# Graph convolution by one-hot products: every summing product split into four of 32 targets, and gathers and sums alternating on TensorE

## The reference, cut to what matters

```python
def gcn_conv(x, W, b, src, dst, n):
    h = x @ W
    deg = jnp.zeros((n,), h.dtype).at[dst].add(1.0) + 1.0
    dinv = jax.lax.rsqrt(deg)
    norm = dinv[src] * dinv[dst]
    agg = jax.ops.segment_sum(h[src] * norm[:, None], dst, num_segments=n)
    return agg + h * (dinv * dinv)[:, None] + b
h = gcn_conv(emb, W1, b1, src, dst, NTOKEN)      # 64 -> 128 wide
nodes = gcn_conv(h, W2, b2, src, dst, NTOKEN)    # 128 -> 64 wide
return nodes[input.reshape(-1)].reshape(b_, l_, NINP)
```

## Time and profile before

| | us |
|---|---|
| median of 3 executions | 2669.42 (2668.12 to 2671.47) |
| span of the profiled execution | 2692.9 |
| PE busy, share of the span | 2076.2, 77% |
| DVE busy | 2301.7, 85% |
| ACT busy | 1927.1, 72% |
| POOL busy | 912.5, 34% |
| chain that ended last: PE L1366 | 28% of the span |
| chain that ended last: PE L1315 | 16% of the span |

### The profile page before, as it was taken

The page is one execution under the profiler, slowest core; times in us unless marked ns, Lnnn a source line. Parts: engine busy times, 40 slices in busy tenths (PEclk is TensorE's granted clock), DMA queues, the critical chain, the costliest instruction groups (busy, mean ns, idle before and its releaser), DMA issues.

```text
span 2692.9 us, 87734 instructions
## 1 busy us (share of the span) xinstructions
PE 2076.2 (77%) x36894; PEld 1728.1 (64%) x36895; DVE 2301.7 (85%) x3711; ACT 1927.1 (72%) x5267; POOL 912.5 (34%) x704
## 2 busy tenths in 40 slices
PE   3455555555562699899999899979999999999990
PEld 2345454444321467787777677868888888888870
DVE  9999999999988688899989999967777777777760
ACT  7869999999663886566666667756777777767760
POOL 2000000000000344435734455414233566655546
PEclk8566666665786899999999999999999999999995
DMA  4000000000021333343446455576888545545431
GB/s 115 0 1 1 1 1 1 1 1 1 19 70 43 106 117 119 123 131 111 106 116 132 120 144 143 143 198 200 245 245 243 153 141 142 142 138 142 135 109 18
DMA packets 191625, 277.10 MB, mean 103 GB/s; under 512 B 122458, under 2 KB 130538, under 8 KB 190972
## 3 DMA queue, kind: packets, MB, share of 16 engines
q1 hardware_dynamic: 168924, 244.05, 28.3%
q0 software_dynamic: 22304, 27.40, 8.4%
HBM read 219.68 MB, written 51.81 MB: 101 GB/s over the span
## 4 chain that ended last, share of the span: by engine, by line
PE 49%; DVE 35%; ACT 7%; issue 4%; POOL 2%; DMA 2%; SPq 0%; another core or an unknown queue 0%; DVEq 0%; POOLq 0%; ACTq 0%
PE ps L1366 28%; PE ps L1315 16%; DVE keys L1610 7%; DVE keys L1611 7%; DVE oh L1946 4%; DVE oh L1460 4%; DVE arena L1460 3%; ACT arena L1118 1%; ACT grow_t L1044 1%; PE ps L1341 1%; PE ps L1251 1%; DVE keys L1630 1%; DVE keys L1631 1%; ACT grow_t L1133 1%; DVE keys L1872 1%
## 5 line engine op out<-in xcount | busy, mean ns | idle before, releaser
L1133 ACT ACTIVATE grow_t<-ps 128x384 bf16<-128x384 f32 x2744 | 1143.6, 499 | 528.5 <-PE ps L1315 491.4
L1366 PE MATMUL ps<-grow_t,oh 128*128 128x192 bf16 x10952 | 1057.9, 248 | 4.7 <-issue 3.5
L1366 PEld LDWEIGHTS ps<-grow_t,oh 128*128 128x128 bf16 x10952 | 880.7, 98 | 128.3 <-issue 111.1
L1946 DVE TENSOR_TENSOR oh<-iorep,dl 128x2048 bf16<-128x2048 bf16 x686 | 832.7, 1218 | 132.4 <-PE ps L1366 103.7
L1315 PE MATMUL ps<-arena,keys 128*32 128x192 bf16 x21952 | 611.4, 249 | 65.9 <-DVE keys L1872 23.8
L1315 PEld LDWEIGHTS ps<-arena,keys 128*32 128x32 bf16 x21952 | 428.7, 97 | 201.6 <-issue 139.8
L951 POOL DMA_INDIRECT zring<-table,sidx x296 | 383.9, 1297 | 497.6 <-PE ps L1315 446.0
L859 POOL DMA_INDIRECT arena<-line,row_i x22 | 29.8, 1354 | 832.1 <-DVEq L1688 825.6
L1044 ACT ACTIVATE grow_t<-colf,arena 128x128 bf16<-128x128 f32 x992 | 294.3, 393 | 7.7 <-PE ps L1179 7.7
L1872 DVE TENSOR_SCALAR keys<-keys,rowf 128x2048 bf16<-128x2048 int16 x344 | 259.7, 755 | 30.3 <-DMA keys<-srel 20.2
L1610 DVE TENSOR_TENSOR keys<-keys 128x1280 f32<-128x1280 f32 (+4 forms) x212 | 246.6, 1163 | 12.6 <-ACT keys L1097 9.4
(11 more groups left out here) (246 smaller groups left out, 1915.0 us busy)
## 6 DMA issues: line engine op xcount, KB each, us to landing
keys<-srel SPq DMA_DIRECT2D x344, 512.0 KB
out<-res SPq DMA_DIRECT2D x50, 512.0 KB
table<-arena SPq DMA_DIRECT2D x19, 384.0 KB, 2.8
table<-sgn_l SPq DMA_DIRECT2D x73, 96.0 KB
arena<-table SPq DMA_DIRECT2D x5, 960.0 KB, 8.5
zring<-table,sidx POOLq DMA_INDIRECT x296
nodes<-arena SPq DMA_DIRECT2D x73, 64.0 KB
arena<-in_L_rec_edge_index SPq DMA_DIRECT2D x2, 1171.5 KB, 5.3
```

The lines of the kernel that those rows point to most:

```text
L1133: act.activation(grow[:, (layer * NB + j) % DEEP, h * 2 * ROW:(h + 1) * 2 * ROW], psum[HALF_BANK[layer][HB * j + h][0]][:, 0:2 * ROW], ACT ...
L1366: mm = pe.matmul(sums(sl, k), dwin[:, (layer * NB + j) % DEEP, t // TT, k * P:(k + 1) * P, t % TT], grow[:, (layer * NB + j) % DEEP, t * R ...
L1946: dve.tensor_tensor(dwin[:, (layer * NB + j) % DEEP, 0:made[1], :, :], iorep[:, :, :].unsqueeze(1).to_broadcast(made), dl_h[:, j * BT:j * ...
```

## The change

In the functions of both layers every product that adds into the targets' rows is cut along the targets: in place of one product of 128 stationary columns there are four of 32 (`WIN` = 4, `ROOM` = 32), each into its own 32 partitions of the same bank, with the same moving rows. This holds for `scatter`, for both kinds of surplus and for `own_rows`; the semaphore is raised by the last of the four. The gathers were of that form already. Transposes and the flag's product in layer one keep theirs. In a batch, the gather of one half now stands directly ahead of the wait and the sums of another: gather 4j+4+h, then sum 4j+h, for h = 0 to 3, where before all four gathers stood ahead of all sums.

```diff
--- before.py
+++ after.py
@@ -1318,13 +1318,18 @@
                     if t % 2:
                         mm.then_inc(gmm, 1)
 
-                def sums(sl, k):
-                    return py[sl % 2][:, k * ROW:(k + 1) * ROW]
+                def add_rows(bank, k, one_hot, rows, first, last):
+                    for q in range(WIN):
+                        mm = pe.matmul(bank[q * ROOM:(q + 1) * ROOM, k * ROW:(k + 1) * ROW], one_hot[:, q * ROOM:(q + 1) * ROOM],
+                                       rows, start=first, stop=last)
+                    return mm
 
                 def own_rows(sl):
                     b = first_block(sl)
                     table_to(min(b + SUP, BLOCKS) - 1)
-                    pe.matmul(py[sl % 2][:, 0:SUP * ROW], ident_h[:, :], xtab[:, b * ROW:(b + SUP) * ROW], start=True, stop=False)
+                    for q in range(WIN):
+                        pe.matmul(py[sl % 2][q * ROOM:(q + 1) * ROOM, 0:SUP * ROW], ident_h[:, q * ROOM:(q + 1) * ROOM],
+                                  xtab[:, b * ROW:(b + SUP) * ROW], start=True, stop=False)
 
                 def rows_in(item):
                     i = place[item]
@@ -1338,8 +1343,7 @@
                         if kind == "o":
                             u = rows_in(item)
                             for k in range(SUP):
-                                mm = pe.matmul(sums(blk, k), ooh[:, out_of[item], k * P:(k + 1) * P], zring[:, u, :],
-                                               start=False, stop=False)
+                                mm = add_rows(py[blk % 2], k, ooh[:, out_of[item], k * P:(k + 1) * P], zring[:, u, :], False, False)
                             mm.then_inc(zmm, 1)
                         else:
                             mini.append(item)
@@ -1350,8 +1354,7 @@
                         ring = [rows_in(item) for item in mini]
                         for k in range(SUP):
                             for n, u in enumerate(ring):
-                                mm = pe.matmul(pt[:, k * ROW:(k + 1) * ROW], ooh[:, out_of[mini[n]], k * P:(k + 1) * P], zring[:, u, :],
-                                               start=(n == 0), stop=(n == 1))
+                                mm = add_rows(pt, k, ooh[:, out_of[mini[n]], k * P:(k + 1) * P], zring[:, u, :], n == 0, n == 1)
                                 if k == SUP - 1:
                                     mm.then_inc(zmm, 1)
 
@@ -1363,9 +1366,9 @@
                     if w == 0:
                         own_rows(sl)
                     for k in range(SUP):
-                        mm = pe.matmul(sums(sl, k), dwin[:, (layer * NB + j) % DEEP, t // TT, k * P:(k + 1) * P, t % TT],
-                                       grow[:, (layer * NB + j) % DEEP, t * ROW:(t + 1) * ROW],
-                                       start=False, stop=(w == CELLS - 1 and k == SUP - 1))
+                        mm = add_rows(py[sl % 2], k, dwin[:, (layer * NB + j) % DEEP, t // TT, k * P:(k + 1) * P, t % TT],
+                                      grow[:, (layer * NB + j) % DEEP, t * ROW:(t + 1) * ROW],
+                                      False, w == CELLS - 1 and k == SUP - 1)
                     if t == BT - 1 or c == ST - 1:
                         mm.then_inc(ymm, 1)
 
@@ -1404,11 +1407,9 @@
                             bank_free(*before)
                             pe.matmul(psum[bank][:, 0:1], ones[:, :], bad_h[:, :], start=True, stop=True).then_inc(bad_mm, 1)
                     surplus(j)
-                    for x in range(HB * j + AHEAD, HB * j + AHEAD + HB):
-                        if x < HB * NB:
-                            gather_half(x)
-
                     for h in range(HB):
+                        if HB * j + AHEAD + h < HB * NB:
+                            gather_half(HB * j + AHEAD + h)
                         pe.wait_ge(evac, HB * layer * NB + HB * j + h + 1 + FREE)
                         for t in (2 * h, 2 * h + 1):
                             scatter(j, t)
```

## The result

The changed kernel takes 3325.88 us (median of 4, 3323.08 to 3329.05) against 2670.44 us for the kernel before on the same chip: 1.2458 times, 95% interval 1.2440 to 1.2476. The profiled execution has a span of 3327.1 us, 634.2 more than that of the kernel before (2692.9 us, which lies 22.5 us above its median; the medians differ by 655).

What follows compares the result with a forecast made beforehand. TensorE was taken to bound layer two alone and layer one together with VectorE. Profiled 2692.9 + 258 + 122 = 3073 us, less 23.5 for the unprofiled median, gave 3050 us; range 2560 to 3450.

Steps and rivals of the forecast that it cites:

- Sign and cause: Whole kernel: slower, chance 0.67, because blocks of TensorE instructions arrive later than the split products use them up.
- the step that was put as the crux: TensorE's instruction supply: two buffers, next 256-instruction block requested on entering the one before; 258 us more in layer two, 122 in layer one.
- The three stalls: Layer two before the change: loads stop mid-gather, resuming at 1903.11, 1945.10 and 2047.34, 1.4 us after a block landed.
- T: Price of one instruction block, 2.36 us plus the wait before its packet: 3.95 us in layer two, 3.84 in layer one.
- three waits: From resumption to the next block's packet at three layer-two stalls: 3.1, 3.1 and 2.1 us, at DMA share 0.80.
- my line: Both layers: packet wait taken proportional to DMA share, so a block costs 2.36 + 3.5 x share us.
- rival A: Instruction supply keeps up: layer two gains 72 us, layer one 30, 2567 us in all; chance 0.27.
- Width changes: TensorE between gathers and sums: each change costs about 0.1 us; removing them saves some 72 us in layer two.
- The new order at no cost: Alternating gathers and sums in a batch adds no wait; ScalarE (681 us at most) and VectorE stay beneath: 0 us.
- Rival C: Sums' weights at every second column don't load four abreast, 166 ns a group: 3360 us; chance 0.06.
- The granted clock: TensorE's clock in the profile afterwards: claimed to be at its upper level; no time given.
- VectorE: Its share in the profile afterwards: claimed to go down; its 828 and 619.8 us of work lie beneath the layers' times.

Runs made afterwards that it cites:

- the pieces by themselves: Kernel before plus five pieces of TensorE-only work behind its end (narrow products, fewer columns, 128-wide products, loop, beside list loads); the first two took 73 and 74 us.
- piece 3: Kernel before plus, behind its end, 640 products 128 wide of 192 columns, 5 blocks of instructions; it used a block in 10.6 us.
- the loop: Kernel before plus, behind its end, a loop with 40 passes over 16 groups of four 32-wide products of 192 columns; 52.98 us without a gap.

## Why the prediction was right, and where it was off

**Sign and cause** were right, by the step that was put as the crux: 16 KB packets of 256 instructions, a block sent for when the one before is entered, 1.4 us from landing to use, one gap a block. The trace of the changed kernel and the pieces by themselves show each part. The three stalls from which the step was read were well chosen: of the 12 idle times over 0.3 us in layer two of the kernel before, just these three stand at the border of a block. The Trainium skill (Runtime: NRT & Kernel Launch, Instruction fetch mechanics) has room for 2048 instructions in one sentence and for two blocks in another; piece 3's packets bear out two blocks. It also calls the crossing of a block mostly hidden; here it is hidden only while a block lasts over 3.7 us. It says that a taken branch forces a fetch if its target isn't in the current window of two pages, and the loop, with a body of 128 instructions and one packet in 52 us, agrees.

**The size** was off: 655 us more where 380 were forecast. The term that was mis-sized is T. I took the wait ahead of a packet as proportional to the DMA share, with 0 as its lower end, and had three waits at one share to fit it by; a line through the origin was a choice without a row. In quiet the wait is 1.3 us, not 0. T was 4.49 us in layer two for 3.95, near the top of my 3.3 to 4.7, and 4.22 in layer one for 3.84. At the share of 0.39 that was measured in both layers, my line gives only 2.36 + 3.5 x 0.39 = 3.73. The measured floor alone gives 270 x 3.74 = 1010 us, 209 above layer two's 801 and 103 above layer one's 907. What is left, 270 x 0.75 = 202 and 270 x 0.48 = 130 us, I put down to traffic; it is the remainder and so closes the sum by its making, but leaving out the lists took 155 of the 202 away. The last 22 us of the miss are of another kind: I subtracted the 23.5 us by which the profiled span of the kernel before lies above its median, and the changed kernel's span lies only 1.2 above its own. By spans the miss is 3327 against 3073. A floor of 3.7 us lies above the 2.99 from which rival A decides, so A, to which I gave 0.27, was not to be had. The three waits of 2.1 to 3.1 us were the only rows for this term, and the lower end of 0 had none; I found no late block in a quiet stretch of the trace of before to set it by. The share of 0.80 beside them was also loose: it is that of 1850 to 2000, and in 2000 to 2100, where the third stall lies, it was 0.86.

**Width changes**: 0.1 us each, right (0.107 measured by the order alone), and the split does remove them.

**The new order at no cost**: right as far as the runs can tell; ScalarE and VectorE stay beneath. The order of before with the split took 1193.4 us in layer one and 1198.8 in layer two, for 1139.1 and 1211.6, on a chip 1% slower, so the order may even have helped layer one.

**Rival C** (weights at every second column): wrong, groups of sums stand at 83 ns. Its 3360 us is closer to the measured time than mine, by chance.

**The granted clock**: I said it would stay at its upper level. It fell to 0.95 and 0.92; the low stretch shown stands behind two gaps of 2.6 us. A block run wholly at the lower level would last 5.1 us, more than T, but the packets show no cost. In layer two the 94 spaces between packets with some time at the lower level were 4.35 us on average and the 175 without any 4.55; in layer one it was 58 at 4.05 and 211 at 4.25.

**VectorE** went down in share, as said, and queue 8 carried 567 packets for the 560 forecast.

## What to carry to other kernels

Before cutting a product into smaller ones, divide the time of a stretch by its instructions: in this kernel straight-line code for TensorE at under 3.7 to 4.5 us for 256 instructions (14 to 18 ns for each) is bound by the bringing of the code, however little the array does. The average over a longer stretch does not protect: one split batch in eight cost 2.5%, with a block wanted only every 5.6 us. About half of that loss is not late blocks, though, but stalls within a block whose cause is open. Gaps put down to "issue" in the midst of a run, 256 instructions apart and about 1.4 us behind a packet of the instruction queue, are its mark, and the loop of 64 pairs tried here is free of it. Idle times at other places in a block are something else, even if they too are put down to "issue".

## What the hardware showed that I had not expected

- T in quiet comes in steps of 0.27 us (3.47, 3.75, 4.02), and is 3.7 us on average with the DMA engines at 0.02.
- A loop of 64 pairs ran 40 times at 83 ns a group with one packet in 52 us.
- The change from 32 to 64 columns leaves the same 0.16 us as that between 32 and 128.
- There is a second kind of stall of TensorE, of 0.6 us and within a block of instructions. In layer one the kernel before has 70 of them (37 us), the changed kernel none. 58 of the 70 begin while GpSimd issues an indirect transfer, for 0.48 of the time.
- Beside large lists alone a block took 4.24 us at a DMA share of 0.64 (2955.9 to 2977.1), in the layers at 0.39 with row fetches and stores among it 4.22 and 4.49. Which kind of transfer delays a packet most was not tried beyond leaving out the lists.
